# A depthwise wavelet convolution whose opening is put in another order: three load queues, statistics first, wider zero matmuls

## The reference, cut to what matters

```
xd = concatenate([x[:, :, 0::2, 0::2], x[:, :, 0::2, 1::2], x[:, :, 1::2, 0::2], x[:, :, 1::2, 1::2]], axis=1)
feats = concatenate([dwconv(xd, w1, 1), dwconv(xd, w3, 3), dwconv(xd, w5, 5)], axis=1)
y = einsum('bchw,oc->bohw', feats, w_proj[:, :, 0, 0])
...
x = x + reference_conv(groupnorm(x, 32 groups), w1, w3, w5, w_proj)
```

## Time and profile before

| | us |
|---|---|
| time, median of 3 runs | 136.77 (136.24 to 138.58) |
| the profiled execution | 136.06 |
| its span on the core | 134.3 |
| PE busy | 125.8 (94%) |
| DVE busy | 125.4 (93%) |
| POOL busy | 115.3 (86%) |
| ACT busy | 109.5 (82%) |

### The profile page before, as it was taken

How to read it: one execution, slowest core, us unless ns; L and a number is a source line. 1 busy time by engine, 2 the same in 40 slices (tenths; PEclk the granted TensorE clock), 3 DMA queues, 4 the chain that set the end, 5 groups by cost and what they waited for, 6 DMA issues and landing times.

```text
span 134.3 us, 1653 instructions
## 1 busy us (share of the span) xinstructions
PE 125.8 (94%) x513; PEld 96.5 (72%) x513; DVE 125.4 (93%) x231; ACT 109.5 (82%) x117; POOL 115.3 (86%) x88
## 2 busy tenths in 40 slices
PE   5999999999999999999999999999999599999860
PEld 5976888888886887688877887688867288768520
DVE  6579899999899999999999999999999999999970
ACT  2589989999999999999999999999999998051000
POOL 6261999999899999999999999999999999999800
PEclk9999999999999999999999999999999999999999
DMA  3999999990080044498797927994789649989546
GB/s 82 273 263 198 198 197 201 200 181 5 2 161 0 0 89 77 41 115 155 163 117 104 195 62 78 99 192 106 78 78 182 135 44 112 110 125 198 119 97 137
DMA packets 35848, 16.68 MB, mean 124 GB/s; under 512 B 34048, under 2 KB 34176, under 8 KB 35456
## 3 DMA queue, kind: packets, MB, share of 16 engines
q0 software_dynamic: 1488, 6.93, 38.6%
q1 hardware_dynamic: 32720, 9.18, 37.0%
q10 hardware_dynamic: 1632, 0.48, 1.7%
HBM read 5.46 MB, written 4.19 MB: 72 GB/s over the span
## 4 chain that ended last, share of the span: by engine, by line
POOL 39%; ACT 20%; DVE 19%; issue 13%; PE 6%; DVEq 1%; POOLq 0%; ACTq 0%
POOL RING_SUM L333 37%; DVE ACC L622 14%; ACT G L430 6%; ACT PROD L468 6%; PE YP L660 3%; DVE ACC L618 3%; ACT HI L420 2%; ACT weff L410 2%; ACT HI L439 2%; ACT LO L441 2%; ACT RING_SUM L459 2%; PE YP L756 1%; DVE F L633 1%; POOL LO L320 1%; DVEq L100 1%
## 5 line engine op out<-in xcount | busy, mean ns | idle before, releaser
L333 POOL TENSOR_TENSOR RING_SUM<-RING_SUM,PROD 128x900 f32<-128x900 f32 (+1 forms) x44 | 90.8, 2075 | 3.3
L622 DVE SCALAR_TENSOR_TENSOR ACC<-G,coef,ACC 128x480 f32<-128x480 f32 (+3 forms) x134 | 83.4, 703 | 0.0
L468 ACT ACTIVATE PROD<-G,coef 128x900 f32<-128x900 f32 (+1 forms) x44 | 43.5, 1049 | 0.0
L696 PE MATMUL YP<-HI,wlo 128*128 128x512 f32 (+1 forms) x146 | 38.1, 413 | 0.0
L696 PE MATMUL YP<-LO,whi 128*128 128x512 f32 (+1 forms) x146 | 36.5, 401 | 0.0
L696 PE MATMUL YP<-HI,whi 128*128 128x512 f32 (+1 forms) x146 | 35.9, 398 | 0.4 <-ACT HI L420 0.4
L696 PEld LDWEIGHTS YP<-HI,wlo 128*128 128x128 f32 x146 | 27.5, 189 | 8.7 <-issue 2.9
L696 PEld LDWEIGHTS YP<-HI,whi 128*128 128x128 f32 x146 | 27.3, 189 | 7.5 <-ACT HI L420 0.8
L696 PEld LDWEIGHTS YP<-LO,whi 128*128 128x128 f32 x146 | 27.5, 189 | 7.1 <-issue 1.0
L430 ACT ACTIVATE G<-X,nbias,rstd 64x1024 f32<-64x1024 f32 x16 | 21.1, 1320 | 0.8 <-DVE nbias L540 0.5
L451 ACT ACTIVATE Y<-YP 64x1024 f32<-64x1024 f32 x14 | 15.3, 1094 | 5.8 <-PE YP L756 5.5
(11 more groups left out here) (66 smaller groups left out, 58.5 us busy)
## 6 DMA issues: line engine op xcount, KB each, us to landing
X<-in_x_dram SPq DMA_DIRECT2D x16, 256.0 KB, 5.9
LO<-G POOLq DMA_DIRECT2D x7, 527.5 KB, 5.3
X<-Y POOLq DMA_DIRECT2D x6, 512.0 KB, 7.3
out_dram<-X SPq DMA_DIRECT2D x12, 256.0 KB, 4.4
out_dram<-X SPq DMA_DIRECT2D x6, 128.0 KB, 2.3
XS<-in_x_dram SPq DMA_DIRECT2D x2, 256.0 KB, 4.0
XS<-in_x_dram SPq DMA_DIRECT2D x1, 512.0 KB, 6.7
out_dram<-X ACTq DMA_DIRECT2D x2, 128.0 KB, 2.6
```

Source lines behind the costliest of these rows:

```text
L333: pool.tensor_tensor(dst, dst, prod(b, k), ALU.add).then_inc(prod_added, 1)
L468: act.activation(prod(b, k), g_tap(b, POOL_OF[b][k + 1]), ACT.Copy, scale=of5(POOL_OF[b][k + 1])).then_inc(prod_ready, 1)
L622: dve.scalar_tensor_tensor(half_part(ACC, tap, h), half_tap(b, tap, h), of5(tap), half_part(ACC, tap, h), ALU.mult, ALU.add).then_inc(acc_ ...
L696: mm = nc.tensor.matmul(dst, w[:, n, :], src, start=start, stop=False, skip_group_check=True)
```

## The change

Loads: the second half of `XS` of image 0 goes first on ACT's queue, ahead of `wp` and `w1`; `w5` and `w3` are issued by POOL as its first two instructions; SP loads the top 17 rows of image 0 ahead of its other rows, with a semaphore of their own (`top_loaded`). POOL makes `ident`, `same` and `mhalf` ahead of `avg`. PE's matmuls on no data are now 20 of 256 zero columns ahead of everything, from the first 256 cleared columns on, and 5 of 512 zero columns after the transposes; then `sum_parts(0)` stands ahead of the coefficients, and these ahead of the transposes. The transposes multiply by the permuted identity, so that their result has its columns in order: ACT copies one block (`wpT`, now 128x128) with no permutation, and DVE reads the two others from PSUM. ACT scales 5 taps, three of them ahead of the top rows and two behind, and POOL 4. `wlo` chunks are made each as its `whi` is there, `spread` of image 1 after them. POOL's first `inv_std` and DVE's `part_bias(0)` come ahead of the weights' steps. The second `combine` moves two taps forward.

```
-WARM = (8, 1, 1, 8)
+WARM = (20, 5)
+WARM_COLS = 256
-ACT_SCALED = 7
+ACT_SCALED = 5
-COMBINE_AT = {(0, 8): (1, 1, 2), (1, 3): (2, 2, PAIRS)}
+COMBINE_AT = {(0, 8): (1, 1, 2), (1, 1): (2, 2, PAIRS)}
...
         def _(sp):
             load_parts(sp, 0, 0, 512, xs_loaded[0])
-            load_parts(sp, 0, 512, 1024, xs_loaded[1])
-            load_image(sp, 0, image_loaded[0])
+            load_image(sp, 0, top_loaded, 0, TOP)
+            load_image(sp, 0, image_loaded[0], TOP, PH)
             load_parts(sp, 1, 0, 1024, xs_loaded[2])
...
         def _(pool):
+            pool.dma_start(w_sb[:, 0:W3_AT], w5.rearrange("c a h w -> c (a h w)")).then_inc(w_loaded, 16)
+            pool.dma_start(w_sb[:, W3_AT:W1_AT], w3.rearrange("c a h w -> c (a h w)")).then_inc(w_loaded, 16)
...
+            inv_std(1, 0, 1)
             pool.wait_ge(wpT_ready, 1)
             pool.wait_ge(coef_copied, 1)
             scale_w5(ACT_SCALED)
-            inv_std(1, 0, 1)
             pool.wait_ge(weff_step, CHUNK)
             pool.tensor_copy(whi[:, 0:CHUNK, :], weff[:, 0:CHUNK, :]).then_inc(whi0_ready, 1)
-            scale_w5(ACT_SCALED + 1)
-            pool.wait_ge(whi0_ready, 1)
-            pool.wait_ge(whi_ready, CHUNKS - 1)
+            for n in range(ACT_SCALED + 1, N_INNER):
+                scale_w5(n)
...
         def _(act):
+            load_parts(act, 0, 512, 1024, xs_loaded[1])
             act.dma_start(wp_sb[:, :], wp.rearrange("o c a b -> o (c a b)")).then_inc(wp_loaded, 16)
-            act.dma_start(w_sb[:, 0:W3_AT], w5.rearrange("c a h w -> c (a h w)")).then_inc(w_loaded, 16)
-            act.dma_start(w_sb[:, W3_AT:W1_AT], w3.rearrange("c a h w -> c (a h w)")).then_inc(w_loaded, 16)
...
-            act.wait_ge(wt_ready, 1)
-            for k in (2, 1, 0):
-                copy_wpT(k)
             act.wait_ge(coef_ready, 1)
             act.activation(coef[:, 0:W1_AT], COEF_PS[:, 0:W1_AT], ACT.Copy).then_inc(coef_copied, 1)
+            act.wait_ge(wt_ready, 1)
+            act.activation(wpT[:, :], WT_PS[:, 2 * P:3 * P], ACT.Copy).then_inc(wpT_ready, 1)
...
-            scale_w5(0, ACT_SCALED)
-            act.wait_ge(coef_ready, 2)
-            act.activation(coef[:, W1_AT:N_COEF], COEF_PS[:, W1_AT:N_COEF], ACT.Copy).then_inc(coef_copied, 1)
+            scale_w5(0, CHUNK)
...
-            act.wait_ge(image_loaded[0], 32)
+            act.wait_ge(top_loaded, 32)
             act.wait_ge(stats_ready, 1)
             high_half(0, TOP, 0, hi_top)
+            scale_w5(CHUNK, ACT_SCALED)
+            act.wait_ge(coef_ready, 2)
+            act.activation(coef[:, W1_AT:N_COEF], COEF_PS[:, W1_AT:N_COEF], ACT.Copy).then_inc(coef_copied, 1)
+            act.wait_ge(image_loaded[0], 32)
             high_half(TOP, PH, 0, hi_bottom)
...
         def _(dve):
-            dve.memset(LO[:, SLOTS - 1, :].bitcast(F32), 0.0).then_inc(low_zero, 1)
+            dve.memset(LO[:, SLOTS - 1, 0:WARM_COLS].bitcast(F32), 0.0).then_inc(low_zero, 1)
+            dve.memset(LO[:, SLOTS - 1, WARM_COLS:S_SIZE].bitcast(F32), 0.0).then_inc(low_zero, 1)
...
-            dve.wait_ge(wpT_ready, 2)
+            dve.wait_ge(wt_ready, 1)
             dve.wait_ge(coef_copied, 1)
+            part_bias(0)
             add_w3(0, 1, 2)
-            part_bias(0)
...
         def _(pe):
-            pe.wait_ge(const_step, 3)
+            pe.wait_ge(low_zero, 1)
             for _ in range(WARM[0]):
-                keep_warm(ident[:, :], P)
-            for n, k in enumerate((2, 1, 0)):
-                pe.wait_ge(permuted, n + 1)
-                mm = nc.tensor.transpose(WT_PS[:, k * P:(k + 1) * P], wp_ph[:, k, :], ident[:, :])
-            mm.then_inc(wt_ready, 1)
+                keep_warm(WARM_COLS)
...
-            for _ in range(WARM[1]):
-                keep_warm(ident[:, :], P)
+            sum_parts(0)
             pe.wait_ge(ident_permuted, 1)
             pe.wait_ge(w_loaded, 32)
             coefficients(0, W1_AT)
-            sum_parts(0)
-            for _ in range(WARM[2]):
-                keep_warm(ident[:, :], P)
+            for n, k in enumerate((2, 1, 0)):
+                pe.wait_ge(permuted, n + 1)
+                mm = nc.tensor.transpose(WT_PS[:, k * P:(k + 1) * P], wp_ph[:, k, :], ident_ph[:, :])
+            mm.then_inc(wt_ready, 1)
+            pe.wait_ge(low_zero, 2)
+            for _ in range(WARM[1]):
+                keep_warm(512)
             pe.wait_ge(w1_loaded, 16)
             pe.wait_ge(coef_copied, 1)
             coefficients(W1_AT, N_COEF)
```

More of the change, by code:

```diff
@@ L276, in _ @@
         def _(pool):
-            pool.memset(ident[:, :], 0.0).then_inc(const_step, 1)
-            pool.memset(avg[:, :], 0.0).then_inc(const_step, 1)
-            pool.wait_ge(const_step, 2)
+            pool.dma_start(w_sb[:, 0:W3_AT], w5.rearrange("c a h w -> c (a h w)")).then_inc(w_loaded, 16)
+            pool.dma_start(w_sb[:, W3_AT:W1_AT], w3.rearrange("c a h w -> c (a h w)")).then_inc(w_loaded, 16)
+            pool.memset(ident[:, :], 0.0).then_inc(ident_step, 1)
+            pool.memset(same[:, :], 0.0).then_inc(stat_const, 1)
+            pool.wait_ge(ident_step, 1)
             pool.affine_select(out=ident[:, :], in_=ident[:, :], compare_op=ALU.not_equal, fill=1.0,
-                               base=0, pattern=[[-1, P]], channel_multiplier=1).then_inc(const_step, 1)
-            pool.affine_select(out=avg[:, :], in_=avg[:, :], compare_op=ALU.not_equal, fill=0.5,
-                               base=0, pattern=[[-1, P]], channel_multiplier=1).then_inc(const_step, 1)
-            pool.memset(same[:, :], 0.0).then_inc(stat_const, 1)
+                               base=0, pattern=[[-1, P]], channel_multiplier=1).then_inc(ident_step, 1)
             for k in range(PARTS):
@@ L290, in _ @@
                                    pattern=[[0, P // C], [-PARTS, C]], channel_multiplier=1).then_inc(stat_const, 1)
+            pool.memset(mhalf[:, :], -0.5).then_inc(mhalf_ready, 1)
+            pool.memset(avg[:, :], 0.0).then_inc(avg_step, 1)
+            pool.wait_ge(avg_step, 1)
+            pool.affine_select(out=avg[:, :], in_=avg[:, :], compare_op=ALU.not_equal, fill=0.5,
+                               base=0, pattern=[[-1, P]], channel_multiplier=1).then_inc(avg_step, 1)
             a = avg[:, :].rearrange("p (b i c) -> p b i c", b=2, i=2)
             for i in range(2):
-                pool.wait_ge(const_step, 4 + i)
+                pool.wait_ge(avg_step, 2 + i)
                 pool.affine_select(out=a[:, :, i, :], in_=a[:, :, i, :], compare_op=ALU.not_equal, fill=0.5,
                                    base=-C * (1 - i), pattern=[[-HALF, 2], [-1, C]],
-                                   channel_multiplier=1).then_inc(const_step, 1)
-            pool.memset(mhalf[:, :], -0.5).then_inc(const_step, 1)
+                                   channel_multiplier=1).then_inc(avg_step, 1)
             def inv_std(n, a, b):
-                pool.wait_ge(const_step, 7)
+                pool.wait_ge(mhalf_ready, 1)
                 pool.wait_ge(stat_step, n)
@@ L409, in scale_w5 @@
                 for n in range(n0, n1):
-                    act.activation(weff[:, n, :], wpT[:, 2, :], ACT.Copy,
+                    act.activation(weff[:, n, :], wpT[:, :], ACT.Copy,
                                    scale=of5(INNER[n])).then_inc(w5_scaled, 1)
-            scale_w5(0, ACT_SCALED)
-            act.wait_ge(coef_ready, 2)
-            act.activation(coef[:, W1_AT:N_COEF], COEF_PS[:, W1_AT:N_COEF], ACT.Copy).then_inc(coef_copied, 1)
+            scale_w5(0, CHUNK)
             def high_half(r0, r1, j, done):
@@ L492, in _ @@
                 if b == 0:
-                    act.activation(weff[:, N_INNER, :], wpT[:, 2, :], ACT.Copy, scale=of5(EXTRA)).then_inc(extra_scaled, 1)
-                    act.activation(whi[:, N_INNER, :], wpT[:, 2, :], ACT.Copy, scale=of5(EXTRA)).then_inc(extra_scaled, 1)
+                    act.activation(weff[:, N_INNER, :], wpT[:, :], ACT.Copy, scale=of5(EXTRA)).then_inc(extra_scaled, 1)
+                    act.activation(whi[:, N_INNER, :], wpT[:, :], ACT.Copy, scale=of5(EXTRA)).then_inc(extra_scaled, 1)
             copy_y(B - 2)
@@ L656, in _, with keep_warm @@
         def _(pe):
-            def keep_warm(tile, n):
-                nc.tensor.matmul(YP[:, 0, 0:n], tile, tile, start=True, stop=True)
-            pe.wait_ge(const_step, 3)
+            zeros = LO[:, SLOTS - 1, :]
+            def keep_warm(n):
+                nc.tensor.matmul(YP[:, 0, 0:n], zeros[:, 0:P], zeros[:, 0:n], start=True, stop=True)
+            pe.wait_ge(low_zero, 1)
             for _ in range(WARM[0]):
-                keep_warm(ident[:, :], P)
-            for n, k in enumerate((2, 1, 0)):
-                pe.wait_ge(permuted, n + 1)
-                mm = nc.tensor.transpose(WT_PS[:, k * P:(k + 1) * P], wp_ph[:, k, :], ident[:, :])
-            mm.then_inc(wt_ready, 1)
+                keep_warm(WARM_COLS)
             def coefficients(c0, c1):
```

(6 more changed lines are left out.)

41 lines of the change are left out of this document (22 added, 19 removed).

## The result

| us | before | changed |
|---|---|---|
| time, median of 20 runs | 136.76 | 137.43 |
| lowest | 135.91 | 136.11 |
| ratio changed to before, 95% interval | | 1.0061 [1.0041, 1.0081] |
| the profiled execution | 136.06 | 139.03 |
| its span | 134.3 | 137.2 |

The change made the kernel slower by 0.6%: less than 2%, but the interval leaves 1 out, the sign is the other than forecast (135.9), and the median is just outside the range (134.9 to 137.4). The profiled execution of 139.03 is the slowest of the 20; the same kernel was profiled again (137.31), and where nothing else is said, sizes come from that one.

The account below looks back on a forecast made before the run. DVE was taken as the bound: its first ring tap, fixed work and idle. Opening 0.0 and the removed wait −0.56 gave 135.5 (profiled base) to 136.2 (median base), middle 135.9 us; range 134.9 to 137.4.

Parts of the forecast that it names:

- What bounds the kernel: Whole kernel: DVE's first ring tap (14.62), its fixed work to 127, its idle of 0.56 us, and an unchanged tail.
- The 0.56: DVE's idle at 34.33 before PE's second `combine`: goes in whole when that moves two taps forward, −0.56 us.
- the opening's 0.0 (−0.3 to +0.36): Start to DVE's first ring tap: scalings 0.95 later, two fewer save 0.59, quicker PE perhaps 0.65; middle 0.0 us.
- The small loads: Opening: `w5` and `w3` leave POOL at 0.7 and 1.5, land at 5.5, and PE needs them at 6.6.
- my 6.62: Opening, PE: the coefficients' matmul goes at 6.62, 0.42 us after the sum over parts at 6.2.
- my 7.7 to 8.3: Opening, sign that the forecast is right: ACT's first scaling starts at 7.7 to 8.3.
- rival 2: Opening: GpSimd's loads or constants come late, held up by DVE's clearing; slower than before, 136.3 to 137.5 us; 20%.
- DVE's slack: Opening: DVE's adds, casts and part statistics done at 14.4, 0.4 us ahead of `G`, costing nothing.
- rival 4: Image 0's first real matmuls: PE at 1.2 GHz, 12 matmuls cost 2.4 us, +1.5 net, 137.8 us; 10%.
- The sign I named: PE's first real (L702) matmuls 0.43 us apart would show a slow PE clock and the forecast wrong.
- The base of the sum: Whole kernel: −0.56 us gives 135.5 from the profiled 136.06, 136.2 from the median 136.77; middle 135.9 given.
- A sooner rstd alone therefore buys nothing: Opening: rstd comes 0.6 us sooner, but ACT reached the top rows 0.4 us behind the bias, so no gain.

Follow-up runs that it names:

- the table entry: Kernel before with only the second `combine` moved from behind tap 3 to behind tap 1 of image 1's LO pass: 0.9944, 135.78 us; repeated, 0.996, 135.33 us.
- the fills: Changed kernel plus seven 256-column zero matmuls between `sum_parts` and coefficients, and eight 512-column ones instead of five after the transposes: 136.49 us, ratio 1.0011.

## Why the prediction was wrong

**What bounds the kernel: right.** The first ring tap plus 111.05 to 111.26 plus DVE's waits behind it gives the last `F` in every profile of the table.

**The 0.56: right.** Predicted −0.56, whole; 111.74 becomes 111.05 to 111.10, the idle is gone in all kernels with the new table, and alone the entry is worth 0.4 to 0.56% (0.6 to 0.7 us of the medians). That is the whole of what the change gained.

**The step that failed is the opening's 0.0 (−0.3 to +0.36).** It is +0.7 to +0.9 with PE quick (15.32, 15.48), +0.91 and +2.06 in the two profiles of the changed kernel. For the second profile the sum is: the new order by itself −0.16 (`G` finished at 14.42 with the loads back, 14.58 before: less than two executions differ by), the loads +0.74 (15.16), the cast +0.37 (15.53, where DVE followed `G` by 0.04 before), together +0.91; behind it PE's clock +0.78 and the table entry −0.56, +1.13 in all, where the last `F` has +1.18. Three terms were wrong.

*The small loads* were taken to land at 5.5 and be needed at 6.6. They landed at 7.2 and were used at 7.36 after a wait of 0.97. The prediction had them leave POOL at 0.7 and 1.5; they left half a microsecond later, at 1.27 and 2.00. It had 5.3 us to landing in hand from the earlier trace rows, struck 0.5 to 1.3 off because they are tiny, and they took 5.0 and 5.2. With the loads back the step went at 6.68, close to my 6.62, and scalings at 7.77, inside my 7.7 to 8.3: the working of the order was sound, its input was not. Nor had I asked what the move of the `XS` half does to `w5` and `w3` wherever they stand. In the kernel before that move alone puts them at 8.43. The place (rival 2, 20%) was right, its cause was not: DVE's clearing plays no part. That its 136.3 to 137.5 holds the measured 137.43 is partly luck, for it counted neither the cast nor the clock. The Trainium skill (DMA: Bandwidth & Descriptors, "Issuing engine by pattern") spoke against the issue from GpSimd. The kernel before with that edit agrees (+0.55%), through 0.73 + 0.58 us of GpSimd's time and a landing of `w3` at 7.0 instead of 6.2; in the changed kernel, where ACT issues them nearly as late, it decides little (0.97 and 0.83 of wait).

*DVE's slack* "done at 14.4, 0.4 ahead of `G`". One cast of 128x384 took 1.10 instead of 0.36. In the kernel that holds `wlo` back it took 0.36 with all else equal, so it is GpSimd's `wlo` subtraction, which now runs beside it, that costs the 0.74. Of that, 0.37 comes through to the ring tap, and 0.61 where `G` comes sooner (loads back). I had asked only whether POOL would be late, not what its earlier work does to DVE. The Trainium skill (SBUF — State Buffer, "SBUF: two separate sides") has it: of a GpSimd instruction and a DVE instruction that needs the port they share, the one that starts first holds it to its end, and the other waits. The trace agrees: the subtraction runs from 13.19 to 14.19, the cast starts at 13.31 and ends at 14.41. The prediction drew on that very section for the wrong pair, the clearing against the descriptors. DVE's adds from PSUM, in the same gap, cost nothing to speak of: three take 0.85 to 0.94, before 0.87 to 0.88.

*PE's clock* (rival 4, 10%). "`PEclk` is 1.00 before" was true of a kernel that had matmuls between all its steps; the change took them out. In 14 of 20 executions of the changed kernel the mean granted clock was below 0.99, and with the fills in this became rare. The sign I named was there (0.42 for a 512-column matmul; I had said 0.43), and the chance was far too low. The price was too high: 2.4 us for twelve matmuls, 1.5 net of slack and of the 0.56. DVE waited 0.78 for it in the second profile and 1.40 in the first, and the 14 executions have a median of 137.47, four others 136.11 to 136.48, so 1.16 (the last two are those of 138.69 and 139.03, with a printed clock of 0.999). DVE felt it little at the first `combine` (0.16), mostly at image 1's sum over parts (0.62 and 1.24), which I had not costed.

**The base of the sum.** 135.9 was the middle between 135.5, which goes with the profiled execution of 136.06, and 136.2, which goes with the median. Medians are compared here, so the prediction's own sum says 136.2; the error in the change itself is the same, −0.56 against +0.67.

**"A sooner rstd alone therefore buys nothing": not refuted.** The variance was ready at 7.0 instead of 8.05 (8.21 less 0.16), yet the bias stood at 8.14 behind a wait of 1.15 for the transposes, which its own new place in DVE's code brings. No run had the sooner variance without that.

**What stays open.** A load of 4.5 KB took from 3.0 to 6.2 us from issue to landing; the runs show that it grows with what is issued ahead of it and beside it, not how the transfers divide between queues, nor why 6.2 in the kernel before and 4.8 in the changed one behind the same two loads. Why the changed kernel's first profile prints a clock of 1.00 where its matmuls take 0.42 each was not followed up. Whether the new order pays once loads, cast and clock are all mended is not shown: no kernel with it was faster than the table entry alone.
